# Attention of a macaron block: the scores for the maxima in two row tiles of TensorE

## The chip, the cores and the metric

The kernel runs on one core of a Trainium2 chip. The metric is the device time of one execution in microseconds (us); the smaller, the better. Five engines work beside one another, each through its own list of instructions in order: TensorE (PE in the profile, its weight loads PEld), VectorE (DVE), ScalarE (ACT), GpSimd (POOL) and SyncE (SP), which here only issues DMAs. They wait for one another by semaphores.

## The reference

The input x is 8 x 512 tokens of 128 numbers. Three sublayers follow each other; the change touches the second alone.

```python
x = x + 0.5 * ffn(layernorm(x))      # mixture of 64 experts, top 8, and a shared expert
x = x + attn(layernorm(x))
x = x + 0.5 * ffn(layernorm(x))

def attn(x):                          # 16 heads of 8 numbers
    Q, K, V = x @ wq + bq, x @ wk + bk, x @ wv + bv
    Q, K, V = [a.reshape(B * 16, S, 8) for a in (Q, K, V)]
    scores = einsum('bqd,bkd->bqk', Q, K) / sqrt(8)
    ctx = einsum('bqk,bkd->bqd', softmax(scores), V).reshape(B, S, E)
    out = ctx @ wo + bo + x
    return layernorm(out) * gamma + beta
```

The reshape without a transpose makes each head of a batch 32 tokens of all 128 columns: 512 query rows of 8 numbers against 512 key rows. A tile of 128 tokens therefore holds four complete heads (the index g of the code), and no tile needs another.

## The kernel before, in words

4096 tokens are 32 tiles (NT). For the attention each tile goes through a pipeline whose stages lie in successive steps of TensorE; step n is the list of work in `step`, with a counter tau from 0 to 15.

- Tile n + 4: its normalised rows are transposed (xT, L1663), then multiplied by the query and key weights (qk, L1668). ScalarE copies the results (L1353, L1360). GpSimd splits queries and keys into three bf16 parts each, p1 + p2 + p3 (`split`), and SyncE stores the parts to DRAM (`stack_store`, L455) and loads them into the stacks q_st and k_st (`stack_load`, L472 to L477). A stack is 72 rows: nine combinations of a query part and a key part, 8 rows each, so that one bf16 matmul with 72 rows of contraction gives the scores to nearly f32. The stacks are a ring of four.
- Tile n + 3: the values (v, L1677), copied by VectorE with their bias (`v_copy`, L811).
- Tile n + 2: the scores, only to find the largest of every query row (`scores`, L1701): 16 matmuls of 128 queries by 512 keys, two at a time into PSUM banks 0/1 or 2/3. VectorE takes the maxima of each two (`row_max`, L1084), eight times per tile. The maxima are split in two bf16 numbers (L1088, L1092).
- Tile n + 1: the maxima are transposed (maxT, L1686), copied by ScalarE (`max_copy`, L1368) and put by SyncE as two more rows under the queries (`max_rows`, L450), against rows of -1 in k_st. So a matmul of 74 rows gives score minus maximum.
- Tile n: the transposed scores (`scores_t`, L1714), 128 keys by 512 queries into banks 4 and 5 in turn, which ScalarE exponentiates (L1431). After each four, at tau 3, 7, 11 and 15, the value products of the four exponentials before them (`pv`, L1723), four f32 matmuls in four column tiles of 32, accumulate in bank 6. Each carries a column of ones, so bank 6 also gets the sums of the exponentials. ScalarE copies bank 6 (`ctx_copy`, L1374); the contexts go through DRAM.
- Tile n - 2: VectorE divides (`ctx_div`, L1097 and L1100), TensorE projects (proj, L1691), VectorE adds the residual (`z_add`, L1106) and takes statistics (L1110).

xT, maxT, qk, v and proj all use PSUM bank 7, in the order of the table `uses`. Each waits (`misc`) until the one before it in that order has been read out: proj(n - 2) until v_copy(n + 3), the next step's xT until z_add(n - 2). A transposed-score matmul waits for the exponential two before it. The scores wait until their banks' maxima have been taken. VectorE's list per step is maximum 0, 1, 2, ctx_div, 3, 4, v_copy, 5, 6, z_add, 7, the split of the maxima, statistics; every fourth step has more work for the layer norm. Before the first step, VectorE fills the k stacks with -1 (L1058), and ScalarE issues the first tile's key loads (`first_keys`, L1411 and L1414).

Of the kernel before, what the change touches and what calls it, by code (L numbers as in the profile page):

```python
# [15 lines left out]
def macaron_kernel(nc, x_in, wq, bq, wk, bk, wv, bv, wo, bo, gamma, beta,  # L16
# [22 lines left out]
    NR = NPART * NPART * HD  # L39
    MR = NR  # L40
# [21 lines left out]
    with ExitStack() as ctx:  # L62
# [139 lines left out]

        def heads(stack, rows, g):

            return stack[rows, g * 512:(g + 1) * 512]
# [108 lines left out]
        s_kini = sem("k_stacks_filled")  # L314
        s_xl = [sem(f"x_reloaded{g}") for g in range(NG)]
# [45 lines left out]
        def _(sp):  # L361
# [84 lines left out]
            def attention():  # L446
# [10 lines left out]

                def stack_load(t, r):

                    if isinstance(t, int) and t == 0:  # L460
                        sp.wait_ge(a_pst, 16)
                        parts = parts_dram[0].rearrange("g c (d j) s -> (c d) g (j s)", d=HD)
                        for b in range(NPART):
                            sp.dma_start(q_st[0][b * NPART * HD:(b + 1) * NPART * HD, :], parts[0:NPART * HD])\
                              .then_inc(a_stk[0], 16)
                        return
                    wait_each(sp, (a_ST, 16 * (t - 3)), (a_pst, 16 * t + 16))
                    parts = parts_dram[r].rearrange("g c (d j) s -> (c d) g (j s)", d=HD)
                    for b in range(NPART):

                        first = b * NPART * HD
                        sp.dma_start(q_st[r][first:first + NPART * HD, :], parts[0:NPART * HD]).then_inc(a_stk[r], 16)  # L472
                        kept = (NPART - b) * HD
                        sp.dma_start(k_st[r][first:first + kept, :], parts[(NPART + b) * HD:2 * NPART * HD])\
                          .then_inc(a_stk[r], 16)
                        if b:
                            sp.dma_start(k_st[r][first + kept:first + NPART * HD, :],  # L477
                                         parts[NPART * HD:(NPART + b) * HD]).then_inc(a_stk[r], 16)
# [72 lines left out]
        def _(pool):  # L551
# [172 lines left out]
            def split(t, r):  # L724

                p1, p2, p3 = [part_r[r % 2].rearrange("p (g qk c s) -> p c qk g s", g=NH, qk=2, c=NPART)[:, c]
                              for c in range(NPART)]
# [67 lines left out]
        def _(dve):  # L795
# [18 lines left out]
            def split(t, r):  # L814

                p1, p2, p3 = [part_r[r % 2].rearrange("p (g qk c s) -> p c qk g s", g=NH, qk=2, c=NPART)[:, c]
                              for c in range(NPART)]
# [45 lines left out]
            def ffn(f):  # L863
# [193 lines left out]
                for i in range(NBUF):  # L1057
                    ins = dve.memset(k_st[i][:, :], -1.0)  # L1058
# [188 lines left out]
        def _(act):  # L1247
# [102 lines left out]
            def attention():  # L1350
# [25 lines left out]
                def step(n, r, end=NT):  # L1376
                    mid = not isinstance(n, int)
                    for tau in range(16):
                        kt, g = tau // 4, tau % 4
                        act.wait_ge(a_ST, 16 * n + (tau + 1))  # L1380
                        if g == 0:
                            wait(act, a_PV, 4 * n + (kt - 1))
                        act.activation(p_r[tau % NPB], bank[4 + tau % 2][:, :], ACT.Exp, scale=SCALE).then_inc(a_P, 1)
                        if tau == 0 and (mid or n + 4 < end):
                            xT_copy(n + 4, r)
                        if tau == 3 and (mid or n + 1 < end):
                            max_copy(n + 1, (r + 1) % NBUF)
                        if tau == 5 and (mid or n >= 1):
                            ctx_copy(n - 1, (r - 1) % NBUF)
                        if tau == 7 and (mid or n + 4 < end):  # L1390
                            qk_copy(n + 4, r)
# [13 lines left out]
                def first_keys():  # L1405
# [3 lines left out]
                    for b in range(NPART):  # L1409
                        first, kept = b * NPART * HD, (NPART - b) * HD  # L1410
                        act.dma_start(k_st[0][first:first + kept, :], parts[(NPART + b) * HD:2 * NPART * HD])\  # L1411
                           .then_inc(a_stk[0], 16)
                        if b:
                            act.dma_start(k_st[0][first + kept:first + NPART * HD, :], parts[NPART * HD:(NPART + b) * HD])\  # L1414
                               .then_inc(a_stk[0], 16)
# [8 lines left out]
                for n in range(NT):  # L1424
                    r = n % NBUF
                    for tau in range(16):
# [7 lines left out]
                        if tau == 3 and n + 1 < NT:  # L1434
                            max_copy(n + 1, (r + 1) % NBUF)
                        if tau == 5 and n >= 1:
                            ctx_copy(n - 1, (r - 1) % NBUF)
                        if tau == 7 and n + 4 < NT:
                            qk_copy(n + 4, r)
                        if tau in (9, 11, 13, 15) and n >= 6 and n % GT == 2:  # L1440
                            z_norm(n - 6 + (tau - 9) // 2)
# [390 lines left out]
```

## Time and profile before

| | us |
|---|---|
| median of 3 runs (lowest, highest) | 841.36 (840.29, 845.68) |
| profiled execution, its own time | 838.61 |
| its span | 836.9 |
| TensorE busy | 671.0 (80%) |
| VectorE busy | 611.7 (73%) |
| ScalarE busy | 460.3 (55%) |
| GpSimd busy | 394.3 (47%) |
| mean granted clock of TensorE | 0.853 |

The span splits in three: the first mixture of experts until about 187 us, the attention until about 640, and the second mixture of experts. Busy time is the union of an engine's instructions. The granted clock is the share of TensorE's full 2.4 GHz; it has the values 1.00 and 0.50 (1.2 GHz), and others are means over a stretch. "Idle before" names what an engine waited for ahead of an instruction.

### The profile page before, as it was taken

The numbers are of one execution on the slowest core, as the hardware profiler recorded it, in microseconds if no ns is written. First come the engines' busy times: TensorE is split into PE (matmuls) and PEld (weight loads), VectorE is DVE, ScalarE is ACT, GpSimd is POOL, SyncE is SP. The second block draws the span as 40 slices with busy tenths as digits, with TensorE's granted clock in tenths as the row PEclk, the third lists the DMA queues.
The fourth block names the chain that finished last, engine by engine and source line by source line (L and its number), as shares of the span: only waits on it lengthen the run. The fifth ranks groups of instructions, "written<-read, shape, count | busy, mean of one in ns | idle before, by whom it ended". The sixth has DMA issues, their size and how long they took to land.

```text
span 836.9 us, 16049 instructions
## 1 busy us (share of the span) xinstructions
PE 671.0 (80%) x5121; PEld 306.4 (37%) x5121; DVE 611.7 (73%) x1572; ACT 460.3 (55%) x1057; POOL 394.3 (47%) x529
## 2 busy tenths in 40 slices
PE   4895666603899999999999999999999768666760
PEld 3643454402233333333333333333323534344540
DVE  4798744446868889899899898998983869853430
ACT  5753222201267778777787778877778644222220
POOL 5575787754523324242343433342301457577762
PEclk9997667755589999999999999999999759676585
DMA  7997443336434453444444454545420211543334
GB/s 197 238 251 207 94 77 63 49 48 138 74 63 78 95 102 82 93 96 98 96 88 93 95 97 81 115 74 110 88 62 24 70 44 36 156 88 63 62 42 113
DMA packets 233765, 80.34 MB, mean 96 GB/s; under 512 B 166920, under 2 KB 226472, under 8 KB 233640
## 3 DMA queue, kind: packets, MB, share of 16 engines
q1 hardware_dynamic: 216844, 66.74, 36.2%
q0 software_dynamic: 12288, 10.49, 8.3%
q10 hardware_dynamic: 4572, 2.39, 1.0%
q8 instruction: 25, 0.41, 0.2%
q14 instruction: 36, 0.29, 0.1%
HBM read 49.94 MB, written 31.49 MB: 97 GB/s over the span
## 4 chain that ended last, share of the span: by engine, by line
PE 47%; DVE 13%; POOL 13%; issue 12%; DMA 6%; ACT 6%; POOLq 0%; ACTq 0%; DVEq 0%; SPq 0%
PE psum L1714 13%; PE psum L1723 12%; PE psum L1701 11%; POOL sums L668 7%; DVE arena L1084 5%; POOL arena L643 4%; DMA sums<-sums_sb,sidx 3%; ACT arena L1431 2%; DMA arena<-dispatch_rows,arena 1%; PE psum L1668 1%; PE psum L1509 1%; DVE arena L905 1%; PE psum L1663 1%; DVE arena L901 1%; DVE arena L1097 1%
## 5 line engine op out<-in xcount | busy, mean ns | idle before, releaser
L1084 DVE TENSOR_REDUCE arena<-psum 128x2 f32<-128x1024 f32 x256 | 309.1, 1218 | 46.5 <-PE psum L1701 43.6
L1431 ACT ACTIVATE arena<-psum 128x512 f32<-128x512 f32 x512 | 285.2, 602 | 102.1 <-PE psum L1714 99.7
L1701 PE MATMUL psum<-arena 72*128 72x512 bf16 x512 | 200.8, 400 | 8.4 <-DMA arena<-qk_parts 6.8
L1714 PE MATMUL psum<-arena 74*128 74x512 bf16 x512 | 197.3, 389 | 4.0 <-ACT arena L1431 2.1
L1723 PE MATMUL psum<-arena 128*32 128x512 f32 x1024 | 137.5, 609 | 0.6
L668 POOL DMA_INDIRECT sums<-sums_sb,sidx x64 | 102.3, 1598 | 41.0 <-issue 19.6
L1714 PEld LDWEIGHTS psum<-arena 74*128 74x128 bf16 x512 | 50.7, 100 | 147.3 <-ACT arena L1431 119.3
L735 POOL CAST arena<-arena 128x256 bf16<-128x256 f32 x30 | 11.9, 396 | 192.5 <-issue 181.0
L643 POOL DMA_INDIRECT arena<-dispatch_rows,arena x64 | 64.4, 1007 | 27.3 <-issue 17.9
L1586 PE MATMUL psum<-ident,arena 128*128 128x128 f32 x64 | 24.4, 395 | 58.4 <-DMA arena<-dispatch_rows,arena 58.3
L1701 PEld LDWEIGHTS psum<-arena 72*128 72x128 bf16 x512 | 50.5, 100 | 39.5 <-DVE arena L1084 7.9
L1014 DVE COPY sums_sb<-psum 128x256 f32<-128x256 f32 x32 | 13.6, 425 | 66.9 <-PE psum L1630 45.9
L1321 ACT ACTIVATE arena<-psum 128x256 f32<-128x256 f32 x32 | 12.3, 384 | 66.4 <-PE psum L1586 66.4
L1327 ACT ACTIVATE arena<-psum 128x192 f32<-128x192 f32 x32 | 10.6, 331 | 62.3 <-PE psum L1596 62.3
L1596 PE MATMUL psum<-wgu_sb,arena 128*32 128x192 f32 x512 | 43.9, 487 | 1.0 <-ACT arena L1321 0.9
L1723 PEld LDWEIGHTS psum<-arena 128*32 128x32 f32 x1024 | 20.3, 108 | 54.7 <-issue 37.6
L1586 PEld LDWEIGHTS psum<-ident,arena 128*128 128x128 f32 x64 | 10.1, 165 | 75.4 <-issue 47.2
L1509 PE MATMUL psum<-rwT,z_sb 128*128 128x64 f32 x128 | 28.3, 397 | 3.8 <-ACT z_sb L1453 3.8
L1663 PE MATMUL psum<-ident,arena 128*128 128x128 f32 x32 | 11.0, 345 | 24.2 <-POOL arena L715 21.3
L1097 DVE RECIPROCAL arena<-arena 128x128 f32<-128x128 f32 x32 | 30.1, 942 | 0.0
L1006 DVE TENSOR_TENSOR arena<-arena,psum 128x192 f32<-128x192 f32 x32 | 11.3, 353 | 25.6 <-ACT arena L1327 24.5
L1353 ACT ACTIVATE arena<-psum 128x128 f32<-128x128 f32 x32 | 8.7, 272 | 38.1 <-PE psum L1663 38.1
(147 smaller groups left out, 1136.5 us busy)
## 6 DMA issues: line engine op xcount, KB each, us to landing
arena<-qk_parts SPq DMA_DIRECT2D x127, 96.0 KB
ctx<-arena SPq DMA_DIRECT2D x32, 256.0 KB, 2.1
qk_parts<-arena SPq DMA_DIRECT2D x32, 192.0 KB, 3.7
arena<-lists SPq DMA_DIRECT2D x16, 256.0 KB, 3.3
sums<-x_sb SPq DMA_DIRECT2D x16, 256.0 KB, 4.3
arena<-ctx SPq DMA_DIRECT2D x64, 64.0 KB, 2.6
arena<-qk_parts SPq DMA_DIRECT2D x62, 64.0 KB
wgu_sb<-in_L_ffn_w_gate SPq DMA_DIRECT2D x8, 384.0 KB, 4.4
```

Source lines behind the costliest of these rows:

```text
L643: pool.indirect_dma_start(out=gat[k % NGB], out_offset=None, in_=xw_dram[f.p], in_offset=bass.IndirectOffsetOnAxis(ap=gidx[:, k:k + 1], ax ...
L668: pool.indirect_dma_start(out=acc_dram[f.p], in_=sum_r[q % 2][:, j * D:(j + 1) * D], in_offset=None, out_offset=bass.IndirectOffsetOnAxis( ...
L1084: dve.tensor_reduce(mx_r[r % 2][:, 2 * p:2 * p + 2], src, X, ALU.max).then_inc(a_mx, 1)
L1097: dve.reciprocal(den2_r[r % 2], den2_r[r % 2]).then_inc(a_rc, 1)
L1431: act.activation(p_r[tau % NPB], bank[4 + tau % 2][:, :], ACT.Exp, scale=SCALE).then_inc(a_P, 1)
L1509: ins = pe.matmul(bank[2 + r][:, j * E:(j + 1) * E], xT_all[:, t * P:(t + 1) * P], rwT[:], start=True, stop=True)
L1586: ins = pe.transpose(bank[0][:, j * P:(j + 1) * P], gat[k % NGB][:, 0:D], ident[:])
L1596: ins = pe.matmul(bank[2 + r][i * HC:(i + 1) * HC, j * 2 * F:(j + 1) * 2 * F], gT[r][:, j * P + i * HC:j * P + (i + 1) * HC], wgu_sb[:, e, :],
L1663: pe.transpose(bank[7][:, 0:P], xn_r[r % 2], ident[:]).then_inc(a_use, 1)
L1701: ins = pe.matmul(bank[tau % 4][:, :], heads(q_st[r], rows, g)[:, qt * P:(qt + 1) * P], heads(k_st[r], rows, g), start=True, stop=True)
L1714: pe.matmul(bank[4 + tau % 2][:, :], keys, heads(q_st[r], rows, g), start=True, stop=True)\
L1723: ins = pe.matmul(bank[6][32 * g:32 * g + 32, :], v_r[r][:, g, kt, :], p_r[(4 * kt + g) % NPB], start=(kt == 0), stop=(kt == 3), tile_posi ...
```

## The change

The maxima's scores are computed with the six leading products of parts (48 rows) in place of nine (72). The stacks are laid out anew in 128 rows: rows 0 to 47 hold the six products, rows 48 to 63 two more and 112 to 119 the last one, rows 120 and 121 the maxima. Rows 64 to 111 repeat the six products for heads 2 and 3: queries in columns of heads 0 and 1, keys in columns of heads 2 and 3, and zeros elsewhere, so that they add nothing to the transposed scores, which take rows 0 to 121 now. One matmul on array rows 0 to 47 computes a 128 x 512 block of head g, a second on rows 64 to 111 the block of head g + 2 (two row tiles of 64 rows).

A loop over p from 0 to 7 replaces the 16 matmuls; both matmuls of a pair write the two banks of one maximum. In a step the pairs 2k and 2k + 1 stand directly behind the value products at tau 4k + 3, where before one matmul stood behind each transposed one. The stack loads are 16 DMAs per tile in place of 8, the transpose of the maxima moves from tau 3 to 5, `ctx_copy` and `max_copy` change places, and the normalisations on ScalarE come in twos. Before the attention the stacks are filled by four memsets of 2048 columns and eight of 1024.

```diff
-    NR = NPART * NPART * HD
-    MR = NR
+    LR = NPART * (NPART + 1) // 2 * HD
+    CR = P // 2
+    ER = CR + LR
+    MR = ER + HD
...
+        PAIRS = ((0, 3, 0), (0, 2, 3 * HD), (0, 1, 5 * HD), (1, 3, 6 * HD), (2, 3, ER))
...
+                def queries_load(t, r):
+                    parts = parts_dram[r].rearrange("g c (d j) s -> (c d) g (j s)", d=HD)
+                    for first, last, row in PAIRS:
+                        n = (last - first) * HD
+                        sp.dma_start(q_st[r][row:row + n, :], parts[first * HD:last * HD]).then_inc(a_stk[r], 16)
+                        if row < LR:
+                            sp.dma_start(q_st[r][CR + row:CR + row + n, 0:QC // 2], parts[first * HD:last * HD, NH // 2:NH, :])\
+                              .then_inc(a_stk[r], 16)
...
                 for i in range(NBUF):
-                    ins = dve.memset(k_st[i][:, :], -1.0)
+                    dve.memset(k_st[i][3 * P // 4:P, :], -1.0).then_inc(s_kset, 1)
+                    dve.memset(q_st[i][CR:ER, QC // 2:QC], 0.0).then_inc(s_kset, 1)
+                dve.wait_ge(s_kset, 2 * NBUF)
+                for i in range(NBUF):
+                    ins = dve.memset(k_st[i][CR:ER, 0:QC // 2], 0.0)
                 ins.then_inc(s_kini, 1)
...
-                    dve.tensor_reduce(mx_r[r % 2][:, 2 * p:2 * p + 2], src, X, ALU.max).then_inc(a_mx, 1)
+                    dve.tensor_reduce(mx_r[r % 2][:, p:p + 9:8], src, X, ALU.max).then_inc(a_mx, 1)
...
-                        if tau == 3 and n + 1 < NT:
+                        if tau == 3 and n >= 1:
+                            ctx_copy(n - 1, (r - 1) % NBUF)
+                        if tau == 5 and n + 1 < NT:
                             max_copy(n + 1, (r + 1) % NBUF)
-                        if tau == 5 and n >= 1:
-                            ctx_copy(n - 1, (r - 1) % NBUF)
...
+                def scores(t, r, p):
+
+                    g, qt = p // 4, p % 4
+                    if p == 0:
+                        pe.wait_ge(a_stk[r], lap(t, r, NBUF, 16 * 16))
+                    wait(pe, a_mx, 8 * t + (p - 1))
+                    low, high = slice(0, LR), slice(CR, ER)
+                    cols = slice(qt * P, (qt + 1) * P)
+                    pe.matmul(bank[2 * p % 4][:, :], heads(q_st[r], low, g)[:, cols], heads(k_st[r], low, g),
+                              start=True, stop=True, tile_position=(0, 0))
+                    pe.matmul(bank[2 * p % 4 + 1][:, :], heads(q_st[r], high, g)[:, cols], heads(k_st[r], high, g + 2),
+                              start=True, stop=True, tile_position=(CR, 0)).then_inc(a_S, 1)
...
-                        if tau == 3 and (mid or n + 1 < end):
+                        if tau == 5 and (mid or n + 1 < end):
                             maxT(n + 1, at(1))
...
                         scores_t(n, r, tau)
-                        if mid or n + 2 < end:
-                            scores(n + 2, at(2), tau)
                         if tau == 3 and (mid or n >= 1):
                             pv(n - 1, at(-1), 3)
                         if tau % 4 == 3 and tau > 3:
                             pv(n, r, tau // 4 - 1)
+                        if tau % 4 == 3 and (mid or n + 2 < end):
+                            scores(n + 2, at(2), tau // 2 - 1)
+                            scores(n + 2, at(2), tau // 2)
```

TensorE before, from tau 12 of a step to the head of the next (L1714 transposed scores, L1701 scores for the maxima, L1723 value products, L1663 the transpose xT; a_misc_read counts the read-outs of bank 7, a_max_ready the maxima taken):

```order
L1714 MATMUL psum<-arena 128x512 [waits a_exp_ready]
L1701 MATMUL psum<-arena 128x512 [waits a_max_ready]
L1714 MATMUL psum<-arena 128x512 [waits a_exp_ready]
L1701 MATMUL psum<-arena 128x512
L1714 MATMUL psum<-arena 128x512 [waits a_exp_ready]
L1701 MATMUL psum<-arena 128x512 [waits a_max_ready]
L1714 MATMUL psum<-arena 128x512 [waits a_exp_ready]
L1701 MATMUL psum<-arena 128x512
L1723 MATMUL psum<-arena 32x512 [waits a_exp_ready]
L1723 MATMUL psum<-arena 32x512 x3
L1663 MATMUL psum<-ident,arena 128x128 [waits a_misc_read,a_xn_ready]
```

In this place the last two pairs of scores stand among the transposed ones, ahead of the value products. TensorE in the change, the same place (L1701 and L1703 are the two matmuls of a pair):

```order
L1714 MATMUL psum<-arena 128x512 [waits a_exp_ready] x4
L1723 MATMUL psum<-arena 32x512 [waits a_exp_ready]
L1723 MATMUL psum<-arena 32x512 x3
L1701 MATMUL psum<-arena 128x512 [waits a_max_ready]
L1703 MATMUL psum<-arena 128x512
L1701 MATMUL psum<-arena 128x512 [waits a_max_ready]
L1703 MATMUL psum<-arena 128x512
L1663 MATMUL psum<-ident,arena 128x128 [waits a_misc_read,a_xn_ready]
```

The four transposed matmuls stand in one row, and the pairs 6 and 7 have moved behind the value products, directly ahead of the transpose. VectorE in the change around the same place (L1098 a maximum, L821 the copy of V, L1120 z_add, L1102 and L1106 the split of the maxima):

```order
L1098 TENSOR_REDUCE arena<-psum 128x2 [waits a_scores_in_psum] x2
L821 TENSOR_TENSOR arena<-psum,bv_sb 128x16x8 [waits a_pv_done,a_misc_written]
L1098 TENSOR_REDUCE arena<-psum 128x2 [waits a_scores_in_psum] x2
L1120 TENSOR_TENSOR z_sb<-psum,z_sb 128x128 [waits a_residual_ready,a_misc_written]
L1098 TENSOR_REDUCE arena<-psum 128x2 [waits a_scores_in_psum]
L1102 CAST arena<-arena 128x16 [waits a_max_ready]
L1106 TENSOR_TENSOR arena<-arena 128x16 [waits a_max_high]
```

VectorE's order is that of before: z_add stands between maximum 6 and maximum 7.

## Rows read from the trace of the kernel before

**Rows 1.** By stretch: busy us (count) of PE, PEld, DVE, ACT, POOL; clock, DMA, GB/s.
```profile
400.00:500.00 100.00, 99.28 (x764) 33.90 (x762) 90.52 (x143) 78.05 (x169) 35.71 (x69) 1.00 0.48 96
```

**Rows 2.** The page's groups of instructions: busy, mean ns of one, idle before, releaser.
```profile
L1084 DVE TENSOR_REDUCE arena<-psum 128x2 f32<-128x1024 f32 x256 | 309.1, 1218 | 46.5 <-PE psum L1701 43.6
L1431 ACT ACTIVATE arena<-psum 128x512 f32<-128x512 f32 x512 | 285.2, 602 | 102.1 <-PE psum L1714 99.7
```

**Rows 3.** Timeline of TensorE: the transpose xT at the head of two steps.
```profile
402.97 0.33 PE L1663 MATMUL psum<-ident,arena 128*128 128x128 f32 x1
...
416.17 0.33 PE L1663 MATMUL psum<-ident,arena 128*128 128x128 f32 x1
```

**Rows 4.** Timeline of TensorE, one step: start, duration, line, shapes.
```profile
403.13 0.38 PE L1714 MATMUL psum<-arena 74*128 74x512 bf16 x1
403.35 0.38 PE L1701 MATMUL psum<-arena 72*128 72x512 bf16 x1
...
404.20 0.39 PE L1714 MATMUL psum<-arena 74*128 74x512 bf16 x1
...
405.13 0.38 PE L1701 MATMUL psum<-arena 72*128 72x512 bf16 x1
405.44 1.06 PE L1723 MATMUL psum<-arena 128*32 128x512 f32 x8
406.44 0.39 PE L1714 MATMUL psum<-arena 74*128 74x512 bf16 x1
...
407.10 0.38 PE L1701 MATMUL psum<-arena 72*128 72x512 bf16 x1
```

**Rows 5.** The same timeline: query/key product, what follows it, V product.
```profile
407.32 0.61 PE L1668 MATMUL psum<-arena,wqk_sb 128*128 128x128 f32 x4
407.77 0.38 PE L1714 MATMUL psum<-arena 74*128 74x512 bf16 x1
...
410.70 0.46 PE L1677 MATMUL psum<-wv_sb,arena 128*32 128x32 f32 x32
```

**Rows 6.** Timeline of ScalarE in the same step.
```profile
403.55 0.60 ACT L1431 ACTIVATE arena<-psum 128x512 f32<-128x512 f32 x1 [1.08 <-PE psum L1714]
...
404.20 1.72 ACT L1431 ACTIVATE arena<-psum 128x512 f32<-128x512 f32 x3
405.82 0.25 ACT L1368 ACTIVATE arena<-psum 32x128 bf16<-32x128 bf16 x1
406.87 1.08 ACT L1431 ACTIVATE arena<-psum 128x512 f32<-128x512 f32 x2 [0.79 <-PE psum L1714]
```

**Rows 7.** Timeline of VectorE in the same step.
```profile
402.09 0.28 DVE L1106 TENSOR_TENSOR z_sb<-psum,z_sb 128x128 f32<-128x128 f32 x1
...
407.52 1.23 DVE L1084 TENSOR_REDUCE arena<-psum 128x2 f32<-128x1024 f32 x1 [0.75 <-PE psum L1701]
...
409.85 2.35 DVE L1084 TENSOR_REDUCE arena<-psum 128x2 f32<-128x1024 f32 x2
```

**Rows 8.** Timeline and chain of waits ahead of the first scores.
```profile
179.57 1.76 DVE L1058 MEMSET arena<- 128x2048 bf16 x1 [0.38 <-issue]
...
187.58 0.29 DVE L1050 BATCH_NORM_STATS2 stats<-x_sb 128x6 f32<-128x128 f32 x1 [5.99 <-DMA x_sb<-sums]
...
201.88 3.90 DMA arena<-qk_parts
```

**Rows 9.** Timeline of SyncE: the first and the last of a tile's 8 stack loads.
```profile
403.31 0.31 SPq L472 DMA_DIRECT2D arena<-qk_parts  x1
...
405.95 0.31 SPq L477 DMA_DIRECT2D arena<-qk_parts  x1
```

**Rows 10.** Busy time by stretch, columns as in rows 1, at the attention's end.
```profile
644.00:648.00 4.00, 3.29 (x21) 0.93 (x24) 0.65 (x2) 2.97 (x6) 0.16 (x1) 1.00 0.00 0
656.00:660.00 4.00, 1.59 (x10) 0.46 (x10) 3.53 (x28) 0.81 (x4) 2.46 (x4) 0.90 0.08 18
```

**Rows 11.** Timeline of TensorE: a score matmul at half clock, in step 0.
```profile
234.20 0.63 PE L1701 MATMUL psum<-arena 72*128 72x512 bf16 x1
```

More of the change, by code:

```diff
@@ new lines, in keys_load @@
+                def keys_load(t, r):
+                    parts = parts_dram[r].rearrange("g c (d j) s -> (c d) g (j s)", d=HD)
+                    for first, last, row in PAIRS:
+                        n = (last - first) * HD
+                        src = (2 * NPART - last) * HD if first == 0 else NPART * HD
+                        sp.dma_start(k_st[r][row:row + n, :], parts[src:src + n]).then_inc(a_stk[r], 16)
+                        if row < LR:
+                            sp.dma_start(k_st[r][CR + row:CR + row + n, QC // 2:QC], parts[src:src + n, NH // 2:NH, :])\
+                              .then_inc(a_stk[r], 16)
@@ L458, in stack_load @@
                 def stack_load(t, r):
+                    wait_each(sp, (a_ST, 16 * (t - 3)), (a_pst, 16 * t + 16))
+                    queries_load(t, r)
                     if isinstance(t, int) and t == 0:
[L461 to L465, printed above, removed]
@@ L466, in stack_load @@
-                        return
[L467 to L478, printed above, removed]
+                        return
@@ L480, in ctx_store @@
+                    keys_load(t, r)
                 def ctx_store(t, r):
@@ L724, in split @@
             def split(t, r):
[L726 to L727 removed]
+                p1, p2, p3 = [part_r[r % 2].rearrange("p (g c s) -> p c g s", g=NH, c=2 * NPART)
+                              [:, c:2 * NPART - c:2 * NPART - 1 - 2 * c] for c in range(NPART)]
                 qk, res = [b[r % 2].rearrange("p (qk g s) -> p qk g s", qk=2, g=NH) for b in (qk_r, res_r)]
@@ L1408, in first_keys @@
                     parts = parts_dram[0].rearrange("g c (d j) s -> (c d) g (j s)", d=HD)
[L1409 to L1414, printed above, removed]
+                    for first, last, row in PAIRS:
+                        n = (last - first) * HD
+                        src = (2 * NPART - last) * HD if first == 0 else NPART * HD
+                        act.dma_start(k_st[0][row:row + n, :], parts[src:src + n]).then_inc(a_stk[0], 16)
+                        if row < LR:
+                            act.dma_start(k_st[0][CR + row:CR + row + n, QC // 2:QC], parts[src:src + n, NH // 2:NH, :])\
                                .then_inc(a_stk[0], 16)
@@ L1691, in proj @@
                     pe.matmul(bank[7][:, 0:D], cT_r[r % 2], wo_sb[:], start=True, stop=True).then_inc(a_use, 1)
-                def scores(t, r, tau):
-                    g, qt = tau // 4, tau % 4
-                    if tau == 0:
-                        pe.wait_ge(a_stk[r], lap(t, r, NBUF, 16 * (3 * NPART - 1)))
-                    if tau % 2 == 0:
-                        wait(pe, a_mx, 8 * t + (tau // 2 - 1))
-                    rows = slice(0, MR)
-                    ins = pe.matmul(bank[tau % 4][:, :], heads(q_st[r], rows, g)[:, qt * P:(qt + 1) * P],
-                                    heads(k_st[r], rows, g), start=True, stop=True)
-                    if tau % 2:
-                        ins.then_inc(a_S, 1)
+                def scores(t, r, p):
[9 more added lines that the diff above has]
+                              start=True, stop=True, tile_position=(CR, 0)).then_inc(a_S, 1)
                 def scores_t(t, r, tau):
```

51 lines of the change are left out of this document (19 added, 32 removed).

## The prediction

> **What bounds the kernel now.** I read the slices of the page, then the busy times of a long stretch of the attention, then the groups of instructions, and last the timeline of one step, engine by engine. From 400 to 500 us [rows 1] TensorE is busy 99% of the time, VectorE 91%, ScalarE 78%, at a granted clock of 1.00. So this part, most of the span, goes at TensorE's pace, and the other two wait for it. The groups say what the others do beside it [rows 2]: 256 maxima on VectorE, 1218 ns each, whose waits end with a maxima matmul (L1701), and 512 exponentials on ScalarE, 602 ns, whose waits end with a transposed-score matmul (L1714).
>
> The timeline gives the period: the transpose L1663, issued once per step, starts at 402.97 and at 416.17, so a quiet step lasts **13.20 us** [rows 3]; every fourth step carries normalisations on top. A "busy" figure there includes the tail of a matmul: the pace is the distance of starts, 0.22 us for a 512-column bf16 matmul although each shows 0.38 [rows 4].
>
> **What the change takes from TensorE.** The maxima's scores become 8 pairs per step instead of 16 matmuls. That two row tiles run side by side no row shows. The nearest are the column tiles of the value products: four f32 products of 512 columns take 1.00 us from start to next start [rows 4], where two f32 products of 128 columns alone take 0.45 [rows 5], so four of 512 would need about 3.6 in a row. I take one 0.22 per pair and keep 0.44 as the other end. At 0.22, 8 x 0.22 = 1.76 us of matmul leave each step. A change of tiling costs: the first value product starts 0.31 instead of 0.22 after the matmul ahead of it [rows 4], 0.09 more. The change adds one such switch per quarter of a step (columns to row tiles to whole array, where it was columns to whole array): 4 x 0.09 = 0.36 back, with 0 and 0.15 per switch as ends. If only this counted, a step would be 1.4 us shorter. The Trainium skill (TensorEngine Tiling, Key Properties) says that changing the tiling mode drains the engine. The tail in [rows 4] is 0.38 - 0.22 = 0.16 us; a whole one per added switch would make 0.64 a step instead of my 0.36, so 0.3 us more per step, 8 us in all.
>
> **What the new order does to the waits.** In before, a transposed-score matmul (ST) and a maxima matmul alternate, so each quarter spreads its four ST over 1.76 us and ScalarE keeps up. Now the four ST stand together and all scores come after the value products. I follow one quiet step from its ST0 at t = 0. Links: ST start to exponential start 0.42 (403.13 to 403.55), exponential start to the ST two later 0.65 (403.55 + 0.60 for itself, the ST at 404.20, 0.05 behind it) [rows 4, 6]; exponentials behind one another 0.49 (two in 1.08) [rows 6]; maxima matmul to VectorE start 0.42 (407.10 to 407.52), a reduce every 1.14 [rows 4, 7].
> *Quarter 1*: exponential 0 at 0.42, ST2 at 1.07, ST3 at 1.56 (exponential 1 at 0.91 + 0.65), 1.72 with the copy of xT between (the next exponential follows 0.65 and not 0.49 behind, 403.55 to 404.20 on ScalarE [rows 6]). Value products 2.03, pairs 3.03 and 3.25, ST4 at 3.25 + 0.22 + 0.09 = 3.56. A plain quarter is therefore 1.56 + 0.31 + 1.00 + 0.44 + 0.09 = **3.40** us, against 4 x 0.44 + 0.09 + 1.00 = 2.85 before: what the pairs save, waiting for ScalarE takes back.
> *Quarter 2*: the query/key product now stands right behind the copy of the maxima, on ScalarE behind exponential 5: 3.56 + 0.42 + 0.49 + 0.49 + 0.25 [rows 6] + 0.05 = 5.26; plus 0.45 [rows 5], ST6 5.71, ST7 5.93, value products 6.24 instead of 5.43: **+0.81**.
> *Quarter 3*: ST8 at 7.77, the V product (0.46 [rows 5]) fits in the wait for exponential 8. On VectorE maximum 2 starts at 7.66, the division of the contexts stands before maximum 3 (2.33 from one to the other, 407.52 to 409.85 [rows 7]), which ends at 11.21. The second pair of this block waits for its banks until 11.26 instead of 10.86: **+0.40**.
> *Quarter 4*: ST12 at 11.57; the output projection waits for the copy of V behind maximum 4, to 12.60, about when ST14 is due. Value products 13.44, the last two pairs 14.44 and 14.66.
> *Next step's head*: here is what decides. The transpose at the head of a step uses PSUM bank 7 and waits for z_add, which empties it of the projection; VectorE runs z_add behind maximum 6. Before, pair 6 was computed by tau 13, z_add ran 402.09 to 402.37 and the transpose at 402.97 did not wait [rows 3, 7]. Now pair 6 starts at 14.44 as next-to-last work of the step: maximum 6 at 14.86, z_add 16.00 to 16.28, transpose 16.33, ST0 at 16.49. Without this wait ST0 would stand at 14.66 + 0.22 + 0.09 + 0.16 = 15.13: **+1.36**.
> Sum: 4 x 3.40 + 0.16 + 0.81 + 0.40 + 0.16 + 1.36 = **16.49 us per step, 3.29 more** than 13.20. The periodic extras I leave as large as they are.
>
> **How many steps.** The wait at the head needs z_add of an earlier step and a transpose to come: heads of steps 3 to 27, 25 x 3.29 = 82.3. Steps 0 to 2 lack it: 3 x 1.9 = 5.8. Steps 28 and 29 compute scores but have no transpose and no query/key product: 4 x 3.40 + 0.40 = 14.0 against 13.20 - 0.16 - 0.45 = 12.6, 2.8 together. Steps 30 and 31 compute no scores and stay. Together **+91**.
>
> **Before the first step.** VectorE fills the stacks by four memsets of 1.76 us with 0.38 between them and then waits 5.99 us for the reloaded x, until 187.58 [rows 8]. Now it has four of that size and eight over half the columns (0.88 + 0.38 each, 10.1 in all): their end moves from 181.3 to 191.4, two short copies follow, and the statistics start near 191.9: **+4.3**. The last first-key load is issued at 201.88 and lands 3.90 later, which starts the scores at 205.83 [rows 8]; 8 issues for 5, about 0.35 apart: **+1.1**.
> At nothing I cost: the 8 added issues on SyncE per step (8 x 0.35 = 2.8 us; the 8 of before go out from 403.31 to 406.26 in a 13.2 us step [rows 9]). The keys are needed over a step later; the row of maxima waits behind them to about 6.0, and is needed at 16.5; without that cover the delay would be 0.7 us. The reload of the contexts keeps its place behind the store of the parts, more than half a step ahead of the division that needs it. The normalisations now run in twos behind exponentials 7, 11 and 15, 0.49 us each, next to lulls of ScalarE.
>
> **Sum.** 838.6 (the profiled execution: 836.9 of span and 1.7 around it) + 91 + 5.4 = 935. The median shown is 2.8 above that execution, so **938 us**. My links are rounded upward in places (v, maxima transposes, ends of column tiling), downward in others: +-0.5 us a step, 925 to 952, is this case's own range.
>
> **Rivals.**
> *The clock falls too* (chance 0.2). In before it held 1.00 with TensorE busy 3.29 us of 644 to 648, and fell when it was busy 1.59 of 656 to 660; the 0.90 there is a fall within the stretch [rows 10]. In my new step the 4 us after the last pair hold 1.4 of wait and then five matmuls with two more waits, about 2 us busy, between these two. For it: every step has such a place. Against: full quarters come right behind. At 1.2 GHz a score matmul shows 0.63 instead of 0.38 [rows 4, 11]: four ST 1.0 more and a part of the value products 0.2, about 1.2 us per fall, one per step on 25 steps: +30, 968; more if it stays down over half steps, 985. The Trainium skill (TensorE: Matmul & The Clock Gate, A second HAM failure mode) tells of just this: short idles between groups that cycle through PSUM banks make the clock oscillate, so it supports this rival and not my 938.
> *Row tiles run one after the other* (0.07): 0.44 more per quarter, 1.76 a step, less the 0.40 for which the second pair of quarter 3 no longer waits and 0.22 at the head, where maximum 6 waits for pair 6 and not for 7: 1.14 on 30 steps, 34 more, 972. Only the value products' column tiles [rows 4] speak against it.
> *The quarters are shorter than I trace them* (0.06): if the exponentials of a quarter hide behind the value products more than two banks seem to allow, a quarter is 3.0 and not 3.4: 1.6 less on 28 steps, 45 less, 893. Before's lulls of 0.8 to 1.1 us on ScalarE around the value products [rows 6] speak against it.
> *Faster* (0.05): if maximum 6 and z_add are out before the head, because VectorE reaches them earlier than traced, and ScalarE runs ahead through the value products, TensorE loses its 1.4 us and VectorE becomes the bound at its 90.5 of 100 us [rows 1], 12.1 a step: 30 x 1.3 = 39 less, 5 more in front, 807. It decides at z_add: pair 6 would have to be done 1.4 us before the head. Only the order speaks against it, and that strictly: z_add stands behind maximum 6, which waits for pair 6.
> *No net change* (0.02): shorter quarters and a z_add that is half in time, 841.
> The rest, 0.60, is the forecast.
>
> **Numbers.** The range takes the forecast's own range, most of the clock case and of the shorter stalls: 905 to 975. A difference of 1% (8 us) is what can be told from no change: slower 0.93, same 0.02, faster 0.05.
>
> **What the trace would show.** Right: starts of the transpose 16.5 us apart; its wait of about 1.4 us released by VectorE's z_add; pairs starting at the same time and 0.22 us per pair; ST2 of a quarter waiting for an exponential; TensorE under 80% busy and VectorE about 75%; four wide and eight half memsets. Wrong: a step under 14 us, VectorE above 90%, a transpose that waits for nothing, or a granted clock well under 1.00 from 300 to 600.

## The result, and the profile after

The changed kernel takes **963.5 us** (median of 4 runs, 960.91 to 966.17); the kernel before took 840.83 in the same comparison. The ratio is 1.145, 95% interval 1.140 to 1.149: slower, as forecast, inside the range of 905 to 975, but 25 us above the forecast of 938. The profiled execution took 963.88, its span is 962.3. Executions of a kernel that took over 1.5% more than its fastest are left out of the medians and ratios below.

The attention's engines no longer work through. The busy time by stretch of the changed kernel (columns as in rows 1) over 100 us, and over one quiet step:

```profile
400.00:500.00 100.00, 75.74 (x568) 20.89 (x567) 67.45 (x104) 61.16 (x130) 25.91 (x48) 0.97 0.36 85
529.34:546.43 17.09, 13.05 (x104) 3.70 (x104) 11.79 (x16) 10.09 (x21) 3.82 (x8) 1.00 0.41 97
```

Against [rows 1] TensorE fell from 99 to 76 of 100 us, VectorE from 91 to 67. In that quiet step at full clock TensorE shows 13.05 us of work in 17.09. Where the rest lies is in the timeline of TensorE in this step:

```profile
529.34 0.33 PE L1663 MATMUL psum<-ident,arena 128*128 128x128 f32 x1 [1.30 <-DVE z_sb L1120]
529.56 0.60 PE L1714 MATMUL psum<-arena 122*128 122x512 bf16 x2
530.64 0.39 PE L1714 MATMUL psum<-arena 122*128 122x512 bf16 x1 [0.47 <-ACT arena L1429]
531.29 0.39 PE L1714 MATMUL psum<-arena 122*128 122x512 bf16 x1 [0.27 <-ACT arena L1429]
531.62 1.06 PE L1723 MATMUL psum<-arena 128*32 128x512 f32 x8
532.61 0.39 PE L1701 MATMUL psum<-arena 48*128 48x512 bf16 x1
532.62 0.39 PE L1703 MATMUL psum<-arena 48*128 48x512 bf16 x1
532.84 0.38 PE L1701 MATMUL psum<-arena 48*128 48x512 bf16 x1
...
533.15 0.39 PE L1714 MATMUL psum<-arena 122*128 122x512 bf16 x1
...
534.86 0.71 PE L1668 MATMUL psum<-arena,wqk_sb 128*128 128x128 f32 x4 [0.83 <-ACT arena L1382]
...
541.32 0.39 PE L1701 MATMUL psum<-arena 48*128 48x512 bf16 x1 [0.58 <-DVE arena L1098]
...
542.64 0.49 PE L1691 MATMUL psum<-wo_sb,arena 128*128 128x128 f32 x2 [0.40 <-DVE arena L821]
...
544.53 0.39 PE L1701 MATMUL psum<-arena 48*128 48x512 bf16 x1
...
546.43 0.33 PE L1663 MATMUL psum<-ident,arena 128*128 128x128 f32 x1 [1.30 <-DVE z_sb L1120]
```

The two matmuls of a pair start together (532.61, 532.62) and the next pair 0.22 us later: the row tiles do run side by side. The bracket at the end of a row is the idle time of the engine ahead of it and who ended it; it counts from the end of the tail of the matmul before. The head of the step waits 1.30 for z_add, two transposed-score matmuls wait 0.47 and 0.27 for exponentials, the query/key product 0.83 for the copy of the maxima, pair 5 0.58 for its banks, the projection 0.40 for the copy of V. No matmul in [rows 4] or [rows 5] has such a bracket.

VectorE in the same step:

```profile
537.36 1.23 DVE L1098 TENSOR_REDUCE arena<-psum 128x2 f32<-128x1024 f32 x1 [1.96 <-PE psum L1703]
538.50 0.94 DVE L1111 RECIPROCAL arena<-arena 128x128 f32<-128x128 f32 x1
539.48 0.65 DVE L1114 TENSOR_TENSOR arena<-arena 128x128 f32<-128x128 f32 x1
540.05 1.21 DVE L1098 TENSOR_REDUCE arena<-psum 128x2 f32<-128x1024 f32 x1
```

Maximum 2 and maximum 3 are 2.69 us apart here and 2.33 in [rows 7]. The difference is the multiplication behind the reciprocal, 0.65 us here; before, it took 0.29 (see the last section).

The time by stage, from the starts of the 32 transposes L1663 (head of step n is the one of tile n + 4). First the rows of that line, before and after; the last numbers are the first and the last start:

```profile
L1663 PE MATMUL psum<-ident,arena x32: 328/328/447, 190.3 to 590.6; 128*128 128x128 f32 x32
```

```profile
L1663 PE MATMUL psum<-ident,arena x32: 299/328/472, 191.7 to 707.0; 128*128 128x128 f32 x32
```

| | before | after | more | forecast |
|---|---|---|---|---|
| start to the head of step 0 | 226.4 | 228.7 | 2.3 | 5.4 |
| steps 0 to 2 | 42.8 | 49.9 | 7.1 | 7.2 |
| steps 3 to 26 (24 steps) | 321.4 | 428.4 | 107.0 | 79.0 |
| head of step 27 to the end | 246.3 | 255.3 | 9.0 | 4.7 |
| span | 836.9 | 962.3 | 125.4 | 96.3 |

The forecast is laid out by these stages: a step is counted here from transpose to transpose, so the first of its 25 waits, at the head of step 3, falls into the row of steps 0 to 2.

Of the 24 steps, a quiet one takes 16.94 to 17.21 us, the one shown 17.09. Those with the statistics of x (n = 15, 23) take 18.1, and nine steps in which the granted clock fell to 0.50 for a part of the step take 1.2 to 1.6 more than a like one at full clock. (The steps with normalisations, n = 8, 12, 16, 20, 24, all have such a fall, and are compared with quiet ones.) Such a fall by the columns of rows 1:

```profile
511.00:512.90 1.90, 1.16 (x5) 0.23 (x4) 1.55 (x8) 1.54 (x4) 0.61 (x2) 1.00 0.52 153
512.90:516.40 3.50, 3.50 (x15) 0.47 (x14) 0.89 (x1) 1.39 (x3) 0.69 (x1) 0.52 0.18 50
```

It follows a wait of 1.69 at the head, and catches the value products and the pairs:

```profile
510.75 0.33 PE L1663 MATMUL psum<-ident,arena 128*128 128x128 f32 x1 [1.69 <-DVE z_sb L1120]
...
512.99 1.93 PE L1723 MATMUL psum<-arena 128*32 128x512 f32 x8
514.86 0.60 PE L1701 MATMUL psum<-arena 48*128 48x512 bf16 x1
```

From the value products' start to the pair's that is 1.87 instead of 1.00.

### The profile page after: what moved, and what is told of

The parts are those of the page before. It is cut to its first block, busy times and chain, and to the rows that moved or that the text cites. A ratio compares the mean times of both kernels' runs of the same rounds, so it can differ in the third digit from the quotient of the medians.

```text
span 962.3 us, 16313 instructions
## 1 busy us (share of the span) xinstructions
PE 673.2 (70%) x5121; PEld 281.4 (29%) x5121; DVE 619.2 (64%) x1580; ACT 466.7 (48%) x1057; POOL 396.3 (41%) x529
## 4 chain that ended last, share of the span: by engine, by line
PE 36%; DVE 20%; issue 14%; POOL 11%; ACT 10%; DMA 7%; POOLq 0%; ACTq 0%; DVEq 0%; SPq 0%
PE psum L1723 11%; PE psum L1714 8%; ACT arena L1429 8%; DVE arena L1098 7%; POOL sums L678 6%; PE psum L1701 5%; DMA sums<-sums_sb,sidx 4%; POOL arena L653 3%; DVE arena L1111 3%; PE psum L1668 2%; PE psum L1691 1%; DVE arena L1114 1%; DMA arena<-dispatch_rows,arena 1%; PE psum L1509 1%; PE psum L1677 1%
## 5 line engine op out<-in xcount | busy, mean ns | idle before, releaser
L1098 DVE TENSOR_REDUCE arena<-psum 128x2 f32<-128x1024 f32 x256 | 307.2, 1218 | 166.3 <-PE psum L1703 166.3
L1429 ACT ACTIVATE arena<-psum 128x512 f32<-128x512 f32 x512 | 281.3, 596 | 191.6 <-PE psum L1714 191.2
L1714 PE MATMUL psum<-arena 122*128 122x512 bf16 x512 | 178.0, 397 | 32.4 <-ACT arena L1429 26.1
L1723 PE MATMUL psum<-arena 128*32 128x512 f32 x1024 | 146.5, 646 | 0.0
L1701 PE MATMUL psum<-arena 48*128 48x512 bf16 x256 | 90.4, 414 | 27.8 <-DVE arena L1098 18.5
L1703 PE MATMUL psum<-arena 48*128 48x512 bf16 x256 | 90.4, 414 | 0.0
L1714 PEld LDWEIGHTS psum<-arena 122*128 122x128 bf16 x512 | 43.0, 99 | 127.6 <-ACT arena L1429 86.5
L653 POOL DMA_INDIRECT arena<-dispatch_rows,arena x64 | 64.8, 1012 | 27.6 <-issue 17.9
L1701 PEld LDWEIGHTS psum<-arena 48*128 48x128 bf16 x256 | 17.1, 95 | 150.7 <-issue 86.7
L1663 PE MATMUL psum<-ident,arena 128*128 128x128 f32 x32 | 11.1, 347 | 57.1 <-DVE z_sb L1120 34.4
L1668 PE MATMUL psum<-arena,wqk_sb 128*128 128x128 f32 x128 | 25.3, 326 | 24.1 <-ACT arena L1382 23.3
L758 POOL TENSOR_SCALAR rstdz<-mvz 128x4 f32<-128x4 f32 (+2 forms) x9 | 2.1, 231 | 86.6 <-DVE mvz L1141 86.6
L1723 PEld LDWEIGHTS psum<-arena 128*32 128x32 f32 x1024 | 20.6, 110 | 39.1 <-issue 38.6
```

Source lines behind the costliest of these rows:

```text
L653: pool.indirect_dma_start(out=gat[k % NGB], out_offset=None, in_=xw_dram[f.p], in_offset=bass.IndirectOffsetOnAxis(ap=gidx[:, k:k + 1], ax ...
L1098: dve.tensor_reduce(mx_r[r % 2][:, p:p + 9:8], src, X, ALU.max).then_inc(a_mx, 1)
L1668: ins = pe.matmul(bank[7][:, i * P:(i + 1) * P], wqk_sb[:, i * D:(i + 1) * D], xTt_r[r % 2], start=True, stop=True)
L1701: pe.matmul(bank[2 * p % 4][:, :], heads(q_st[r], low, g)[:, cols], heads(k_st[r], low, g), start=True, stop=True, tile_position=(0, 0))
L1703: pe.matmul(bank[2 * p % 4 + 1][:, :], heads(q_st[r], high, g)[:, cols], heads(k_st[r], high, g + 2), start=True, stop=True, tile_position ...
L1714: pe.matmul(bank[4 + tau % 2][:, :], keys, heads(q_st[r], rows, g), start=True, stop=True)\
```

## Experiments

Theory A is the prediction's: the new order makes waits. Rivals: the row tiling itself costs (B), the clock is most of it (C).

**z_add ahead of maximum 6.** The largest wait of the forecast, taken away.

```diff
-                        if p == 6 and n >= 2:
+                        if p == 5 and n >= 2:
                             z_add(n - 2)
```

> The changed kernel with one move on VectorE: z_add stands ahead of maximum 6 instead of behind it. Theory A (the order makes the waits): the wait at the head of each step (1.30 us in the profile of the change) goes, 25 x 1.3 = 33 us, and some falls of the clock with it, another 3 to 6: 925 us, steps of 15.8 us. Theory B (the row tiling itself, its switches and its longer stacks, makes the kernel slow): the wait at the head is only where time shows up, another takes its place, 955 to 963 us. Theory C (the clock is most of it): falls of the clock go away and no more, 955.

Measured: 915.93, ratio to before 1.089 (1.082 to 1.095). That is 47.6 us less than the change, where 38 were expected. TensorE around the head of a step:

```profile
513.33 0.38 PE L1701 MATMUL psum<-arena 48*128 48x512 bf16 x1
513.33 0.38 PE L1703 MATMUL psum<-arena 48*128 48x512 bf16 x1
513.64 0.33 PE L1663 MATMUL psum<-ident,arena 128*128 128x128 f32 x1
```

The transpose follows 0.31 behind the last pair, without a wait. Quiet steps last 15.66 instead of 17.09: 1.43 x 25 = 36 us. Steps 3 to 26 hold three falls of the clock instead of nine, 6 x 1.5 = 9. B and C are both refuted as main causes: nothing took the wait's place, and the clock alone is not 48 us.

**One row tile.** The second matmul of a pair on the same array rows.

```diff
-                    pe.matmul(bank[2 * p % 4 + 1][:, :], heads(q_st[r], high, g)[:, cols], heads(k_st[r], high, g + 2),
-                              start=True, stop=True, tile_position=(CR, 0)).then_inc(a_S, 1)
+                    pe.matmul(bank[2 * p % 4 + 1][:, :], heads(q_st[r], low, g + 2)[:, cols], heads(k_st[r], low, g + 2),
+                              start=True, stop=True, tile_position=(0, 0)).then_inc(a_S, 1)
```

> The changed kernel with both matmuls of a pair on array rows 0 to 47, so that they cannot run side by side; same values, same order. Theory A: the second starts 0.22 us after the first, 0.44 more per quarter, less 0.22 at the head and what VectorE's waits hide: 1.1 us a step, 30 us more, 993. Theory B: without a second row tile the pairs flow as well or better, 963 or less.

Measured: 1042.43, ratio 1.239 (1.227 to 1.251), so 79 us more than the change; 30 were expected. Theory B is refuted. Quiet steps at full clock take 17.91, which is 0.82 more than in the change and not 1.1: 20 us on 24 steps. TensorE at the end of one such step:

```profile
507.11 0.39 PE L1701 MATMUL psum<-arena 48*128 48x512 bf16 x1
507.34 0.38 PE L1703 MATMUL psum<-arena 48*128 48x512 bf16 x1
507.56 0.38 PE L1701 MATMUL psum<-arena 48*128 48x512 bf16 x1
507.77 0.38 PE L1703 MATMUL psum<-arena 48*128 48x512 bf16 x1
509.23 0.33 PE L1663 MATMUL psum<-ident,arena 128*128 128x128 f32 x1 [1.08 <-DVE z_sb L1120]
```

Four starts 0.22 apart where the change has two. Most of the rest is the clock. In steps 3 to 26, thirteen have a stretch at half clock and take 19.0 to 26.5 us; against like steps at full clock they are 64 us longer in sum, where the nine falls of the change make 13. So about 50 of the 79 us are half clock. The same stretch as above reads

```profile
400.00:500.00 100.00, 85.01 (x454) 22.98 (x454) 52.99 (x84) 49.65 (x105) 19.58 (x38) 0.76 0.28 66
```

that is 0.76 at 85% busy, where the change held 0.97 at 76%.

**Row tiles in the old order.** The order undone, all else kept; the transpose and copies back at their places too.

```diff
                         scores_t(n, r, tau)
+                        if tau % 2 and (mid or n + 2 < end):
+                            scores(n + 2, at(2), tau // 2)
...
-                        if tau % 4 == 3 and (mid or n + 2 < end):
-                            scores(n + 2, at(2), tau // 2 - 1)
-                            scores(n + 2, at(2), tau // 2)
```

> The changed kernel with the order of before: pair p stands behind transposed-score matmul 2p + 1, the transpose and the copy of the maxima back at tau 3. Row tiles, stacks and DMAs as in the change. Theory A: the waits at the head, of the query/key product and of pair 5 go; TensorE has 1.76 us less matmul and 16 switches of 0.09 to 0.16 us more per step (1.4 to 2.6), so steps of 13.0 to 14.0 and 835 to 860 us. Theory B: more switches than in the change, so slower than it, over 963.

Measured: 840.04, ratio 0.997 (0.993 to 1.000). The whole loss is gone with the order; stacks of 122 rows, 16 loads per tile and the longer fill cost nothing that shows. But the tiles bring nothing either: the quiet step is again 13.20. TensorE:

```profile
408.46 0.39 PE L1701 MATMUL psum<-arena 48*128 48x512 bf16 x1
...
408.78 0.71 PE L1668 MATMUL psum<-arena,wqk_sb 128*128 128x128 f32 x4
...
411.71 0.39 PE L1701 MATMUL psum<-arena 48*128 48x512 bf16 x1
411.71 0.39 PE L1703 MATMUL psum<-arena 48*128 48x512 bf16 x1
412.03 0.46 PE L1677 MATMUL psum<-wv_sb,arena 128*32 128x32 f32 x32
412.42 0.71 PE L1714 MATMUL psum<-arena 122*128 122x512 bf16 x2
413.06 0.39 PE L1701 MATMUL psum<-arena 48*128 48x512 bf16 x1
413.06 0.39 PE L1703 MATMUL psum<-arena 48*128 48x512 bf16 x1
413.38 1.06 PE L1723 MATMUL psum<-arena 128*32 128x512 f32 x8
```

From a pair to the next matmul it is 0.32 us, and ahead of a pair it is the same: two transposed-score matmuls and the switch take 0.54 (407.92 to 408.46). Before the query/key product that is 0.10 more than in the kernel before (0.22, from 407.10 to 407.32 in [rows 4] and [rows 5]); this is the switch of the prediction, 0.09, measured into and out of row tiles. Ahead of the value products it is nothing new, since 405.13 to 405.44 in [rows 4] is 0.31 too. Each step has 16 switches around the pairs, and in five of them (four times to value products, once to V) the kernel before switched as well. Eleven are new, and take 1.1 of the 1.76 us saved. The other 0.6 to 0.7 I find, by the distances of starts in this step, in small delays ahead of transposed-score matmuls, about 0.2 at most each, and 0.1 more at the query/key product and at the projection. No run separates these.

**The order alone.** The kernel before, with the new order and no row tiles.

```diff
-                        if mid or n + 2 < end:
-                            scores(n + 2, at(2), tau)
...
+                        if tau % 4 == 3 and (mid or n + 2 < end):
+                            for i in range(tau - 3, tau + 1):
+                                scores(n + 2, at(2), i)
```

> The kernel before with the order of the change alone: 72-row scores without row tiles, four of them behind each group of value products, the transpose and copy of the maxima at tau 5. Theory A (the order makes the waits): quiet steps of 17.9 us, those of the one-row-tile kernel, since rows and stacks cost TensorE nothing; with a share of half-clock stretches as large as there, 1000 to 1050 us. Theory B (row tiles, longer stacks and 16 loads per tile cost of themselves): clearly under the change's 963, near 870.

Measured: 1063.2, ratio 1.260 (1.252 to 1.267), above the interval given. The profile is of an execution of 1119.65, so only its full-clock steps are read: quiet ones take 17.72 us, about the 17.9 expected. Its rows show the waits of the change without any row tile:

```profile
337.64 0.71 PE L1668 MATMUL psum<-arena,wqk_sb 128*128 128x128 f32 x4 [0.83 <-ACT arena L1368]
...
349.55 0.33 PE L1663 MATMUL psum<-ident,arena 128*128 128x128 f32 x1 [1.08 <-DVE z_sb L1106]
```

So the order alone costs some 222 us. Its waits at full clock are about half of that: a quiet step is 4.52 longer than before, about 113 us on 25 steps (an estimate). The rest I put down to the clock, whose mean is 0.77 to 0.79 in these executions against 0.85 in before. Given this order the change, with six products in two row tiles, is 100 us faster; 15 of them are shorter steps at full clock (24 x 0.63), and most of the others again time at half clock.

**The smaller waits.** To the kernel with the early z_add, first the transpose and copy of the maxima at tau 4, then also the division behind maximum 1.

```diff
-                        if tau == 5 and (mid or n + 1 < end):
+                        if tau == 4 and (mid or n + 1 < end):
                             maxT(n + 1, at(1))
...
-                        if tau == 5 and n + 1 < NT:
+                        if tau == 4 and n + 1 < NT:
                             max_copy(n + 1, (r + 1) % NBUF)
```

> The change with z_add ahead of maximum 6 (916 us), and in addition the transpose and the copy of the maxima at tau 4, so that the query/key product no longer stands right behind them. Theory A: its wait of 0.83 us shrinks to about 0.3, 0.5 us on 27 steps: 900 to 905 us, quiet steps of 15.1. Rival: the exponentials of the quarter come later by the copy, and the step keeps 15.66.

```diff
-                        if p == 2 and n >= 2:
+                        if p == 1 and n >= 2:
                             ctx_div(n - 2, at(-2))
```

> The same, and in addition ctx_div behind maximum 1 instead of maximum 2. Theory A: pair 5 no longer waits 0.58 us for its banks, v_copy and the projection come earlier too: 0.6 to 0.9 us a step, 880 to 890 us, quiet steps near 14.4, which is four bare quarters of 3.4 plus the transpose. Rival: the wait moves to ScalarE's side and less than 0.3 a step is won.

Measured: 903.43 (ratio 1.074, 1.068 to 1.079) and 886.25 (1.053, 1.047 to 1.058), quiet steps 15.33 and 14.92. Both times are as expected, with some luck in it. In the first, the wait ahead of the query/key product shrank only to 0.62, so a quiet step won 0.33 and not 0.5; one fall of the clock less in steps 3 to 26 did the rest. In the second, the quiet step is 0.5 above its 14.4, since the projection now waits 0.76 for the copy of V, but the steps with statistics lost a whole microsecond and the clock held 1.00 through steps 3 to 26. TensorE in the second:

```profile
500.92 0.71 PE L1668 MATMUL psum<-arena,wqk_sb 128*128 128x128 f32 x4 [0.62 <-ACT arena L1382]
...
506.42 0.39 PE L1701 MATMUL psum<-arena 48*128 48x512 bf16 x1
...
506.64 0.38 PE L1701 MATMUL psum<-arena 48*128 48x512 bf16 x1
...
508.33 0.49 PE L1691 MATMUL psum<-wo_sb,arena 128*128 128x128 f32 x2 [0.76 <-DVE arena L821]
```

Pair 5 (506.64) stands 0.22 behind pair 4 (506.42), its wait is gone. Two of the forecast's links are thus taken out and one is shortened, from 963.5 to 886. What is left of the loss is 45 us, 1.72 a quiet step: four transposed-score matmuls in a row, whose third waits for ScalarE, and the two waits that stay, 0.62 and 0.76.

**Pairs in the middle of a quarter.** If TensorE waits for ScalarE behind the second transposed-score matmul anyway, the pairs fit there.

```diff
                         scores_t(n, r, tau)
+                        if tau % 4 == 1 and (mid or n + 2 < end):
+                            scores(n + 2, at(2), tau // 2)
+                            scores(n + 2, at(2), tau // 2 + 1)
```

> The changed kernel with both pairs of a quarter directly behind its second transposed-score matmul, where TensorE waits for ScalarE anyway, and the maxima's transpose and copy at tau 3. Theory A: the two pairs with their switches (0.62 us) fill the wait of 0.63, a quarter is 2.9 to 3.1 us, z_add is done before the head, VectorE (12 us a step of work) becomes the bound or nearly: steps of 12.6 to 13.2, 815 to 840 us. Theory B: 940 or more, since tiles and switches are those of the change plus 4 switches a step.

Measured: 835.31, ratio 0.992 (0.989 to 0.995): just under before, by less than 1%. Quiet steps 12.95 to 13.11; pair 5 still waits for its banks:

```profile
408.42 0.39 PE L1701 MATMUL psum<-arena 48*128 48x512 bf16 x1 [0.41 <-DVE arena L1098]
```

**VectorE's other work behind the blocks.** To that kernel:

```diff
-                        if p == 2 and n >= 2:
+                        if p == 1 and n >= 2:
                             ctx_div(n - 2, at(-2))
...
-                        if p == 4 and n + 3 < NT:
+                        if p == 5 and n + 3 < NT:
                             v_copy(n + 3, at(3))
...
-                        if p in (5, 6) and n >= 7 and n % GT == 3:
-                            x_stats((n - 7) // GT, 2 * (p - 5), 2 * (p - 4))
+                        if p == 5 and n >= 7 and n % GT == 3:
+                            x_stats((n - 7) // GT)
```

Besides, z_var moves from p 0 to 1 and x_var behind the split of the maxima.

> The kernel with the pairs in the middle of a quarter (835 us, quiet steps of 12.95), with VectorE's other work moved to behind the second maximum of a block, where it no longer keeps two banks waiting: ctx_div and z_var behind maximum 1, v_copy and all four x_stats behind maximum 5, x_var behind the split of the maxima. Theory A: the wait of 0.41 us of pair 5 and the ones behind x_stats go; quiet steps of 12.3 to 12.6, 815 to 825 us. Rival: VectorE is busy 93% and already the bound, so only its order changes and 830 to 837 us stay.

Measured: **821.44, ratio 0.976 (0.972 to 0.980)**, the fastest of all. Quiet steps 12.27 to 12.59. By stretch:

```profile
400.00:500.00 100.00, 97.60 (x820) 28.44 (x820) 94.23 (x148) 83.49 (x181) 38.49 (x74) 1.00 0.49 113
```

**What the row tiles are worth there.** The same kernel with one row tile (the edit of above), and the nine products of before with all four score matmuls at tau 4k + 1 and the same VectorE order.

> The best kernel so far (821 us: pairs in the middle, VectorE's other work behind the blocks) with both matmuls of a pair on array rows 0 to 47, one after the other. Theory A: TensorE is now the bound or close to it, so the second row tile is worth nearly its whole 0.44 us per quarter less the wait for exponential 0 that the pairs fill: 0.2 to 0.4 a quarter, 0.8 to 1.6 a step, 845 to 865 us. Rival: VectorE (94% busy) sets the pace and the row tiles bring nothing: 821 to 828.

> The kernel before (nine products, 72 rows, no row tiles, its own stacks and loads) with all four score matmuls of a quarter behind its second transposed-score matmul, and VectorE's order of the 821 us kernel. Theory A: without row tiles this order wins little, since four matmuls (0.87 us) overfill the wait of 0.63: 13.0 to 13.4 a step, 832 to 846 us. Rival: order alone makes the gain, 821 to 828.

Measured: 856.78 (ratio 1.017, 1.011 to 1.024), steps of 13.81; and 835.63 (0.992, 0.988 to 0.995), quiet steps of 12.91. The second row tile is worth 35 us, as theory A says, and VectorE was not the bound. For the nine products the expectation of time held, but the step came 0.1 under its interval: the order helps them as well. So of the 20 us of the best kernel about 6 come from the order and 14 from six products in two row tiles. The one-tile kernel has as many score matmuls as the nine products and runs none side by side; its step is 0.90 longer, which fits eight switches of 0.10.

## Why the prediction was right, and where it was short

- **The bound of before and what the change takes from TensorE**: right. The pair takes 0.22, a switch 0.10 and not a whole tail of 0.16.
- **The wait at the head**: right in place, releaser and size, and confirmed by taking it away. From the last pair (544.75) to the transpose it is 1.68, and 0.31 without a wait: 1.37, against the 1.36 forecast. It is the largest single part: of the 48 us won without it, 36 are its 25 waits.
- **The other waits**: the query/key product at +5.30 behind ST0 (forecast 5.26), the value products of quarter 1 at 2.06 (2.03). Pair 5 was mis-sized: 2.69 between maxima 2 and 3 instead of 2.33, since the multiplication took 0.65. The query/key product added 0.13 (0.04 later, and 0.54 instead of 0.45 to the next start), and small differences some 0.1, so a quiet step came to 17.09, not 16.49. On 24 steps that is 14 us. The projection waited 0.40, but the matmuls behind it waited for exponentials anyway, as forecast.
- **The clock rival** was given 0.2 and held in part. It fell in nine of steps 3 to 26 and not in each, 13 us in sum (of the 107 that the 24 steps take more), 1.2 to 1.6 a fall. I had priced a fall at 1.2 and taken none into the forecast. These two terms make the 28 us by which the 24 steps exceed the forecast; the periodic work on top of that cancels (statistics of x 0.7 longer, the normalisations of ScalarE hidden). The measured 963.5 lies nearer to this rival's 968 than to my 938, but by luck: its 30 us of falls were about half as much, and the mis-sized step made up for them.
- **The end of the attention**: 9.0 against 4.7. Steps 27 and 30 hold a fall of the clock each, and step 30, which I had left as it was, took 15.5 us from its first exponential to that of step 31, where before it took 12.1.
- **Ahead of the attention**: forecast 5.4, measured 2.3, of which 1.8 was there already when VectorE's fill began (174.19 against 172.35). A half-size fill took 0.48 and not 0.88, so the fill ended at 188.5 where 191.4 was forecast, and the statistics, which now wait for no x, began at 188.99 against 187.58.
- **Shorter quarters, serial row tiles, faster**: all refuted by the rows above: quarter 1 took 3.59 us with the copy of xT (529.56 to the next transposed scores at 533.15; forecast 3.56), and pairs start side by side.
- **The signs**: as forecast, but for the period (17.1 and not 16.5) and VectorE, which was 67% busy and not 75%.

## What to carry to other kernels

Before work is moved behind other work in one engine's list, follow every resource that its consumer releases later (a bank, a buffer that passes a queue of users) to the next one who waits for it: here one z_add behind one maximum cost 1.37 us a step, as much as the row tiles could give at best (1.4). Concurrency in the array pays where the tile's work fills a wait that exists anyway, and its switches are few; alternated one by one, the switches and small delays ate all of it. And when an engine has slack only between blocks, put its side work there, not between the two instructions that release a block's buffers.

## What the runs showed of the hardware that was not expected

- The granted clock did not follow the busy share. In 400 to 500 us it was 0.97 at 76% busy (the change), 0.76 at 85% (one row tile), and 0.61 at 89% in the order alone (the execution of 1119.65):

```profile
400.00:500.00 100.00, 89.46 (x416) 24.03 (x415) 46.40 (x72) 43.89 (x92) 19.10 (x37) 0.61 0.25 49
```

  Part of the busy share is an effect of the half clock. At full clock all three idle alike, 3.3 to 4.0 us of a quiet step; the two slow ones run their score matmuls one after the other. Which property decides was not tested.
- VectorE's multiplication was held up by an instruction of GpSimd. It took 0.65 at the median in the change, and 0.29 in before and in the kernels where it meets no such instruction (row tiles in the old order, pairs in the middle, early division):

```profile
L1114 DVE TENSOR_TENSOR arena<-arena x24: 293/648/657, 271.5 to 682.8; 128x128 f32<-128x128 f32 x24
```

  In the change it falls on GpSimd's split of queries and keys; with one row tile it starts later within the same instruction and takes 0.44:

```profile
539.30 0.68 POOL L751 TENSOR_TENSOR arena<-arena 128x256 bf16<-128x256 f32 x1
```

```profile
501.68 0.67 POOL L751 TENSOR_TENSOR arena<-arena 128x256 bf16<-128x256 f32 x1
502.06 0.44 DVE L1114 TENSOR_TENSOR arena<-arena 128x128 f32<-128x128 f32 x1
```

  Both end 0.15 us behind the end of GpSimd's instruction (539.48 + 0.65 against 539.30 + 0.68, and 502.50 against 502.35). So do all 25 that start within L751 in the change, at 0.145 to 0.149, and the 25 in the kernel with the early z_add: the later the start, the shorter it looks. In before, 30 of its 32 start outside any GpSimd instruction and take 0.29. In the fastest kernel seven start beside GpSimd's power of 128 x 4 numbers (L760) and still take 0.29. No run moved the split alone.
- A fill of 48 rows by 1024 bf16 zeros took 0.48 us, one of 32 rows by 2048 bf16 of -1 took 1.76; the first appears in the trace as 512 elements of 32 bits.

```profile
175.10 1.76 DVE L1068 MEMSET arena<- 32x2048 bf16 x1 [0.48 <-issue]
177.03 0.48 DVE L1069 MEMSET arena<- 48x512 uint32 x1 [0.16 <-issue]
```
